# Attention on one core: row maxima from a 36-row product, two matmuls in the two row halves of the array

## The chip, the cores and the metric

The program runs on one core of a Trainium2 chip. The metric is the device time of one execution in microseconds (us), the median of several. TensorE does the matmuls, VectorE reductions and copies, ScalarE exponentials, GpSimd elementwise work; SyncE issues the DMAs.

## The reference

One transformer block with conditioning, in float32: x is [2, 2048, 576], 16 heads of width 36, MLP width 2304.

```
ada = silu(c) @ W_ada + b_ada                       # six shifts, scales and gates
h = layernorm(x) * (1 + scale_msa) + shift_msa
q, k, v = split(h @ W_qkv + b_qkv)                  # 16 heads of 36
attn = softmax(einsum('blhd,bmhd->bhlm', q * 36**-0.5, k))
x = x + gate_msa * (attn @ v @ W_proj + b_proj)
h = layernorm(x) * (1 + scale_mlp) + shift_mlp
x = x + gate_mlp * (gelu(h @ W_fc1 + b_fc1) @ W_fc2 + b_fc2)
```

The change is in the attention: 2 batches of 16 heads make 32 heads, each with a 2048 x 2048 matrix of scores.

## The kernel before

The program runs in phases: `phase_qkv` (to 423 us of the profile), `phase_attention` (424 to 2338 us), `phase_proj`, `phase_mlp`. Every engine has its instructions in program order; they meet in semaphores.

**Operands.** q and k are stored as a high part and a low part (`qkh`, `qkl`). For a head, `qs` and `ks` hold 108 rows: high, low, high of q against high, high, low of k, so one matmul over 108 rows sums the three products. Rows 108 and 109 of `qs` hold the negative row maximum in two parts, against ones in `ks`; a matmul over 110 rows gives the scores less their row maximum. Three heads are held (`NB` = 3).

**Row maxima (units).** `score_max` (line 1207) multiplies 128 queries with 512 keys over 108 rows into one of four PSUM banks `sp`; VectorE's `tensor_reduce` (line 1269) takes the maximum over the 512. A head has 64 units. They run ahead: `THERE` = 80 units are done in `phase_qkv`, the other 1968 in attention, eight in a batch. When a head's units are done, `row_max`, a transpose on TensorE (line 1213) and two small operations on VectorE make the two rows of maxima, which SyncE writes into `qs`.

**Scores.** `scores_t` (line 1224) multiplies 128 keys with 512 queries over 110 rows into one of three banks `st`; ScalarE's exponential (line 1326) writes `pt`. Tile x goes to bank x % 3. `bank_free` makes its weight load wait until the exponential of tile x - 3 is done. From tile `X0`, when no units are left, the scores have six banks.

**Value products.** `products` (line 1237) multiplies 128 keys by 37 columns of v (36 and a one for the sum) with two halves of `pt`, the pair (a = 0, 1) in the column halves of the array, into one bank `op`. Each matmul is float32 and stands in the trace as two records. After eight pairs (a block) ScalarE and VectorE copy the bank out (lines 1334 and 1302), GpSimd adds the halves, SyncE stores them.

**Order.** The list `plan` sets the order on every engine. A batch b is eight score tiles. TensorE runs unit, score, unit, score, ... (eight of each), and then the four value products (16 records) of batch b - 1. There are 256 batches; 246 of them carry units.

Of the kernel before, what the change touches and what calls it, by code (L numbers as in the profile page):

```python
# [7 lines left out]
F = mybir.dt.float32  # L8
# [8 lines left out]
H = 16  # L17
# [12 lines left out]
NH = B * H  # L30

# [353 lines left out]
def phase_qkv(nc, A, ident, adaT, eps, bq, sc, qs0, ks0, qs1, ks1, hh0, lo0, mx, nm, mh, ml, gd, xf, cond, W_ada,  # L385
# [127 lines left out]
    def sync(e):  # L513
# [59 lines left out]
        def first_loads():  # L573
            e.wait_ge(s_on, 3)
            e.wait_ge(s_qo[0], 32 * tiles_before(HCH * NF))
            e.wait_ge(s_qo[1], 32 * tiles_before(HCH * NF + 1))
            for dst, src, r in ((qs0, qkh, 0), (qs0, qkl, 36), (qs0, qkh, 72), (ks0, qkh, 0), (ks0, qkh, 36),
                                (ks0, qkl, 72)):
                f0 = C if dst is ks0 else 0
                e.dma_start(dst[r:r + D, :].bitcast(F), src[f0:f0 + D, 0:L]).then_inc(s_q0, 16)  # L580

        def second_loads():
            e.wait_ge(s_mm, UN * (NCH - 1))
            e.wait_ge(s_q0, 96)
            e.dma_start(ks1[108:110, :].bitcast(F), ks0[108:110, :].bitcast(F)).then_inc(s_q1, 16)
            for dst, src, r in ((qs1, qkh, 0), (qs1, qkl, 36), (qs1, qkh, 72), (ks1, qkh, 0), (ks1, qkh, 36),
                                (ks1, qkl, 72)):
                f0 = D + (C if dst is ks1 else 0)
                e.dma_start(dst[r:r + D, :].bitcast(F), src[f0:f0 + D, 0:L]).then_inc(s_q1, 16)
# [50 lines left out]
        e.wait_ge(s_q0, 96)  # L640
        e.wait_ge(s_q1, 112)
        e.wait_ge(s_m, 32)

    def tensor(e):
# [33 lines left out]
        def score_max(n):  # L678
            h, k = divmod(n, 64)
            qb, k4, q, kk = k // 4, k % 4, (qs0, qs1)[h], (ks0, ks1)[h]  # L680
            if n < 2:
                e.wait_ge(s_row, 12)
                e.wait_ge(s_q0, 96)
            else:
                e.wait_ge(s_mx, n - 1)
            if n == 64:
                e.wait_ge(s_mh, 2)
                e.wait_ge(s_q1, 112)
            e.matmul(sp[n % 2][:, :], q[0:108, qb * 128:qb * 128 + 128], kk[0:108, k4 * 512:k4 * 512 + 512],
                     start=True, stop=True).then_inc(s_s, 1)  # L690
# [329 lines left out]
def phase_attention(nc, A, W, tile, ident, qs0, ks0, qs1, ks1, mx, nm, mh, ml, gd, W_proj, b_proj, xf, qkh, qkl, vd,  # L1020
# [12 lines left out]
    NP = 8  # L1033
    G = NH * 32
    NBAT = G // 4
    NBLK = G // 8
    W0 = 24
    LAST = NBAT - 8
    INV = NBLK // 2 + 6
    THERE = 80  # L1040
    X0 = 64 * NH - THERE
# [3 lines left out]
    ks = [ks0, ks1, A.sb("ks2", [128, L], R)]  # L1045
    vs = [A.sb(f"vs{i}", [128, 16, VW]) for i in range(2)]
# [4 lines left out]
    sp = [A.ps(f"sp{i}", [128, 512]) for i in range(4)]  # L1051
# [11 lines left out]
    for b in range(NBAT + 1):  # L1063
        s = Step()
        s.b, s.last = b, None
        s.late = plan[-1].last if plan else None
        s.slot = None
        if s.late is not None:
            s.slot = len(slots)
            slots.append(("mh", s.late))  # L1070
        s.units = [[] for _ in range(8)]
        for i in range(min(8, NH * 64 - todo)):
            s.units[i].append((todo, len(slots)))
            slots.append(("mx", todo))
            todo += 1
            if todo % 64 == 0:
                s.last = todo // 64 - 1
        s.turn = b - LAST - 1 if LAST < b <= LAST + KT else None
        s.now = b - 1 if 0 < b <= NBAT else None
        s.block = (b - 3) // 2 if b > 2 and b % 2 else None  # L1080
        plan.append(s)

    def slot_free(e, k):

        if k > 3:
            kind, n = slots[k - 4]
# [6 lines left out]
    spare = (len(slots) - 1) % 4  # L1093
    six = [st[(X0 + j) % 3] for j in range(3)] + [sp[j] for j in range(4) if j != spare]

    def bank(x):

        return st[x % 3] if x < X0 else six[(x - X0) % 6]

    def bank_free(e, x):  # L1100
        if x < X0 + 3:
            if x > 2:
                e.wait_ge(s_p, x - 2)
        elif x < X0 + 6:
# [12 lines left out]
    def weight(b):  # L1117

        j, r = divmod(b - W0, 4)
        return divmod(j, KT) if 0 <= j < 2 * KT and r == 0 else (None, None)  # L1120

    def sync(e):
        def load(h):
            i, b, hd = h % NB, h // H, h % H
            sl = slice(b * L, (b + 1) * L)
            if h >= NB:
                e.wait_ge(s_st, 64 * (h - 2))
            if h == H:
                tile.stored(e)
            for dst, src, r in ((qs, qkh, 0), (qs, qkl, 36), (qs, qkh, 72), (ks, qkh, 0), (ks, qkh, 36),  # L1130
                                (ks, qkl, 72)):
                f0 = hd * D + (C if dst is ks else 0)
                e.dma_start(dst[i][r:r + D, :].bitcast(F), src[f0:f0 + D, sl]).then_inc(s_qk[i], 16)
# [12 lines left out]

        load_v(0)
# [6 lines left out]
        for s in plan:  # L1154
# [7 lines left out]
            if s.b < NBAT:  # L1162
                h, r = divmod(s.b, 8)
                if r == 0 and h + 2 < NH:
                    load(h + 2)
                if r == 2 and h + 1 < NH:
                    load_v(h + 1)
# [19 lines left out]
        for i in range(NB):  # L1187
            e.wait_ge(s_qk[i], 96 * len(range(i, NH, NB)) - (96 if i < 2 else 0))
            e.wait_ge(s_m[i], 32 * len(range(i, NH, NB)) - (32 if i == 0 else 0))
        e.wait_ge(s_one, 16)  # L1190
# [10 lines left out]
    def tensor(e):  # L1201
        def score_max(n, slot):
            h, k = divmod(n, 64)
            qb, k4, i = k // 4, k % 4, h % NB
            loaded(e, h)
            slot_free(e, slot)
            e.matmul(sp[slot % 4][:, :], qs[i][0:108, qb * 128:qb * 128 + 128], ks[i][0:108, k4 * 512:k4 * 512 + 512],  # L1207
                     start=True, stop=True).then_inc(s_s, 1)

        def max_rows(h, slot):  # L1210
            e.wait_ge(s_nm, h)
            slot_free(e, slot)
            e.transpose(sp[slot % 4][0:16, 0:128], nm[:, :], ident[:, :]).then_inc(s_mt, 1)

        def scores_t(x):
            h, u, kb = x // 64, (x // 16) % 4, x % 16
            i = h % NB
            if x % 64 == 0:
                if h == 2:
                    e.wait_ge(s_one, 16)  # L1220
                loaded(e, h)
                rows_there(e, h)
            bank_free(e, x)
            e.matmul(bank(x)[:, :], ks[i][0:110, kb * 128:kb * 128 + 128], qs[i][0:110, u * 512:u * 512 + 512],  # L1224
# [16 lines left out]
        def turn(kt):  # L1241
# [5 lines left out]
            e.matmul(sp[spare][:, :], W.sel[:, kt, :], W.rr[:, 0, :], start=True, stop=True).then_inc(W.s_ta, 1)  # L1247

        for s in plan:
            if s.late is not None:  # L1250
                max_rows(s.late, s.slot)
            for q in range(8):
                for n, slot in s.units[q]:
                    score_max(n, slot)
                if s.b < NBAT:
                    scores_t(8 * s.b + q)
            if s.turn is not None:
                turn(s.turn)
            if s.now is not None:
                for q in range(4):  # L1260
                    products(4 * s.now + q)

    def vector(e):
        def score_max(n, slot):
            k = n % 64
            e.wait_ge(s_s, n - THERE + 1)
            if k < 2:
                e.wait_ge(s_nm, n // 64 - 1)
            e.tensor_reduce(mx[:, k // 4, k % 4:k % 4 + 1], sp[slot % 4][:, :], AX.X, ALU.max).then_inc(s_mx, 1)  # L1269

        def row_max(h):
            e.wait_ge(s_mx, 64 * (h + 1) - THERE)
# [21 lines left out]
        for s in plan:  # L1294
            if s.late is not None:
                max_rows(s.late, s.slot)
# [6 lines left out]
            for q in range(8):  # L1303
                if (s.b, q) == (0, 5):
                    tile.low(e)
                for n, slot in s.units[q]:
                    score_max(n, slot)
                    if n % 64 == 63:
                        row_max(n // 64)
# [4 lines left out]
            if s.turn is not None:  # L1314
                e.wait_ge(W.s_ta, s.turn + 1)
                e.wait_ge(W.s_a[0], 48)
                e.tensor_tensor(W.oi[:, s.turn, :], sp[spare][:, :], W.oi[:, s.turn, :], ALU.mult).then_inc(
                    W.s_u, 1)

    def scalar(e):  # L1320
        def exps(x):
# [4 lines left out]
            e.activation(pt[g % NP][:, a * 512:a * 512 + 512], bank(x)[:, :], ACT.Exp, scale=SCALE).then_inc(s_p, 1)  # L1326

        for s in plan:
# [20 lines left out]
    def gpsimd(e):  # L1349
# [36 lines left out]
        for s in plan:  # L1386
# [820 lines left out]
```

## Time and profile before

| | |
|---|---|
| median of 3 runs | 3413.26 us (3413.03 to 3413.68) |
| profiled execution, from first to last instruction | 3411.2 us |
| granted TensorE clock | 1.00 throughout |
| TensorE busy | 3398.5 us |
| VectorE busy | 1978.2 us |
| ScalarE busy | 1498.0 us |
| attention with units (246 batches) | 424.03 to 2275.51 us |
| attention without units | 2275.51 to 2338.31 us |

The profile gives for the profiled execution the span only; all runs lie 1.8 to 2.5 us above it. A matmul's recorded length holds its way through the array, so two of them in a row overlap in the records: what a matmul costs is the distance between the starts of two neighbours.

### The profile page before, as it was taken

How to read it: one execution, taken by the hardware profiler on the slowest of the kernel's cores; microseconds unless marked ns; L12 is line 12 of the kernel's file. 1: busy time of each engine (PE TensorE's matmuls, PEld its weight loads, DVE VectorE, ACT ScalarE, POOL GpSimd, SP SyncE). 2: the span in 40 equal slices, each digit the busy share in tenths (PEclk: the TensorE clock that was granted, in tenths of full speed). 3: DMA queues.
4: the chain of work that ended last, by engine and by line, in shares of the span. 5: the costliest groups of instructions: out<-in, count | busy, mean ns of one | idle time of the engine just before them, and what ended most of it. 6: DMA issues, size and time to landing. Idle time of an engine off the chain costs nothing. (4 is left out here: it accounts for less than half of the span.)

```text
span 3411.2 us, 46656 instructions
## 1 busy us (share of the span) xinstructions
PE 3398.5 (100%) x17032; PEld 2270.5 (67%) x17032; DVE 1978.2 (58%) x3591; ACT 1498.0 (44%) x2806; POOL 361.5 (11%) x283
## 2 busy tenths in 40 slices
PE   9999999999999999999999999999999999999999
PEld 7888845545545545544554554547988989898988
DVE  6447577766776776776776676754643343423332
ACT  3322355555555555555555555566531111212120
POOL 0000010111100000010000000015610101000000
PEclk9999999999999999999999999999999999999999
DMA  7563421212112121111212112114751212421211
GB/s 230 177 186 115 153 74 30 65 41 61 38 34 51 31 55 30 45 43 33 55 31 51 34 31 54 31 39 153 267 173 51 80 49 91 126 84 47 76 55 53
DMA packets 132596, 266.15 MB, mean 78 GB/s; under 512 B 17475, under 2 KB 39491, under 8 KB 125458
## 3 DMA queue, kind: packets, MB, share of 16 engines
q1 hardware_dynamic: 132374, 263.17, 25.8%
q8 instruction: 142, 2.33, 0.3%
q14 instruction: 80, 0.66, 0.1%
HBM read 164.64 MB, written 97.26 MB: 77 GB/s over the span
## 5 line engine op out<-in xcount | busy, mean ns | idle before, releaser
L1269 DVE TENSOR_REDUCE q_mx<-b_sp 128x1 f32<-128x512 f32 x1968 | 1196.4, 676 | 228.2 <-PE b_sp L1207 228.2
L1326 ACT ACTIVATE b_pt<-b_st 128x512 f32<-128x512 f32 x2009 | 1013.4, 626 | 441.5 <-PE b_st L1224 434.2
L1237 PE MATMUL b_op<-b_pt,b_vs 128*37 128x512 f32 x4096 | 929.4, 596 | 0.0
L1237 PEld LDWEIGHTS b_op<-b_pt,b_vs 128*37 128x37 f32 x4096 | 223.7, 113 | 567.5 <-issue 440.4
L2073 PE MATMUL d_pm<-d_vh,d_ah 128*128 128x288 f32 x1152 | 339.3, 295 | 0.6 <-DVE d_al L2111 0.6
L2074 PE MATMUL d_pm<-d_vl,d_ah 128*128 128x288 f32 x1152 | 339.3, 295 | 0.0
L2075 PE MATMUL d_pm<-d_vh,d_al 128*128 128x288 f32 x1152 | 339.2, 294 | 0.0
L1392 POOL TENSOR_TENSOR w_oc<-b_oa,b_ob 37x512 f32<-37x512 f32 x127 | 163.0, 1284 | 1589.1 <-DVE b_ob L1302 1583.1
L1207 PE MATMUL b_sp<-q_hh,q_lo 108*128 108x512 f32 x688 | 284.1, 413 | 0.9 <-PEq L1011 0.9
L1224 PE MATMUL b_st<-q_qs,q_ks 110*128 110x512 f32 x697 | 275.7, 397 | 0.0
L1224 PE MATMUL b_st<-q_lo,q_hh 110*128 110x512 f32 x672 | 263.9, 397 | 0.0
L1207 PE MATMUL b_sp<-q_ks,q_qs 108*128 108x512 f32 x640 | 263.7, 412 | 0.0
L1207 PE MATMUL b_sp<-b_ks,b_qs 108*128 108x512 f32 x640 | 263.7, 412 | 0.0
L1302 DVE COPY b_ob<-b_op 37x512 f32<-37x512 f32 x127 | 86.7, 683 | 292.4 <-PE b_op L1237 292.4
L1224 PE MATMUL b_st<-b_qs,b_ks 110*128 110x512 f32 x640 | 253.3, 396 | 0.0
L1334 ACT ACTIVATE b_oa<-b_op 37x512 f32<-37x512 f32 x127 | 75.6, 595 | 347.9 <-PE b_op L1237 347.9
L2073 PEld LDWEIGHTS d_pm<-d_vh,d_ah 128*128 128x128 f32 x1152 | 216.1, 188 | 1.5 <-issue 0.9
L2074 PEld LDWEIGHTS d_pm<-d_vl,d_ah 128*128 128x128 f32 x1152 | 216.1, 188 | 0.7
L2075 PEld LDWEIGHTS d_pm<-d_vh,d_al 128*128 128x128 f32 x1152 | 216.2, 188 | 0.0
L2122 DVE TENSOR_TENSOR d_ug<-d_pm,d_gt 128x288 f32<-128x288 f32 x128 | 58.5, 457 | 243.3 <-PE d_pm L2075 243.2
L1207 PEld LDWEIGHTS b_sp<-q_hh,q_lo 108*128 108x128 f32 x688 | 130.1, 189 | 103.1 <-issue 76.2
L1207 PEld LDWEIGHTS b_sp<-q_ks,q_qs 108*128 108x128 f32 x640 | 121.1, 189 | 94.1 <-issue 71.1
(415 smaller groups left out, 4665.9 us busy)
## 6 DMA issues: line engine op xcount, KB each, us to landing
qkh<-a_th SPq DMA_DIRECT2D x72, 256.0 KB, 2.0
qkl<-a_tl SPq DMA_DIRECT2D x72, 256.0 KB, 2.1
d_yi<-y SPq DMA_DIRECT2D x64, 288.0 KB, 3.0
n_oi<-hw SPq DMA_DIRECT2D x12, 1024.0 KB, 5.8
vd<-a_vx SPq DMA_DIRECT2D x8, 1184.0 KB, 6.6
b_vs<-vd SPq DMA_DIRECT2D x32, 296.0 KB, 2.8
a_x<-in_x SPq DMA_DIRECT2D x8, 1152.0 KB, 6.4
ot<-w_oc SPq DMA_DIRECT2D x128, 72.0 KB
```

The costliest lines, as they stand in the source:

```text
L1207: e.matmul(sp[slot % 4][:, :], qs[i][0:108, qb * 128:qb * 128 + 128], ks[i][0:108, k4 * 512:k4 * 512 + 512], start=True, stop=True).then_i ...
L1224: e.matmul(bank(x)[:, :], ks[i][0:110, kb * 128:kb * 128 + 128], qs[i][0:110, u * 512:u * 512 + 512], start=True, stop=True).then_inc(s_st, 1)
L1237: ins = e.matmul(op[64 * a:64 * a + VW, :], vs[h % 2][:, 2 * j + a, :], pt[g % NP][:, a * 512:a * 512 + 512], start=j == 0, stop=j == 7)
L1269: e.tensor_reduce(mx[:, k // 4, k % 4:k % 4 + 1], sp[slot % 4][:, :], AX.X, ALU.max).then_inc(s_mx, 1)
L1302: e.tensor_copy(ob[i][:, :], op[0:VW, :]).then_inc(s_oa, 1)
L1326: e.activation(pt[g % NP][:, a * 512:a * 512 + 512], bank(x)[:, :], ACT.Exp, scale=SCALE).then_inc(s_p, 1)
L1334: e.activation(oa[i][:, :], op[64:64 + VW, :], ACT.Copy).then_inc(s_oa, 1)
L1392: e.tensor_tensor(oc[i][:, :], oa[i][:, :], ob[i][:, :], ALU.add).then_inc(s_oc, 1)
L2073: e.matmul(out, ah[:, f, ts], vh[:, f, cs], start=f == 0, stop=False)
L2074: e.matmul(out, ah[:, f, ts], vl[:, f, cs], start=False, stop=False)
L2075: ins = e.matmul(out, al[:, f, ts], vh[:, f, cs], start=False, stop=f == NT - 1)
L2122: e.tensor_tensor(ug[m % 2][:, :], pm[m % 4][:, 0:HALF], gt[:, b, cs], ALU.mult).then_inc(s_ug, 1)
```

## The change

- `rows_of` orders the 108 rows anew: high q against high k stands in rows 0 to 35, high q against low k in rows 64 to 99, and low q against high k in rows 36 to 63 and 100 to 107. A head takes eight DMAs where it took six. A ninth loads `km`: the high part of k for keys 1024 to 2047, in rows 64 to 99 (two buffers). Its wait in `load` is for the units of the head that used the buffer.
- A unit is now 128 queries by 1024 keys in two matmuls over 36 rows: rows 0 to 35 of `qs` with `ks` (the first 1024 keys), rows 64 to 99 of `qs` with `km` (the second 1024). They write the two banks of one PSUM tile `sp2` of 1024 columns. One `tensor_reduce` takes both maxima. The maximum is that of the high parts' product alone. A head has 32 units. 40 are there before attention (`phase_qkv` still makes them with 80 matmuls over 108 rows), 984 are left.
- `sp` was four banks for four units; `sp2` is two tiles for two units. The scores keep their three banks, the value products their one.
- `plan` goes in half-batches hb of four score tiles: TensorE runs two units, four scores, and the two value products of hb - 1. There are 512 half-batches; hb 1 to 492 carry units. `NP`, the number of `pt` buffers, is 6 where it was 8.

On TensorE, within a head in the middle of attention (`b_sp` banks of the units, `b_st` banks of the scores with their number, `b_s_p` the exponentials' semaphore). Before, a piece of a batch's sixteen:

```order
L1207 MATMUL b_sp0<-q_ks0,q_qs0 128x512 [waits b_s_mx,b_s_qk0]
L1224 MATMUL b_st1<-b_qs2,b_ks2 128x512 [waits b_s_p]
L1207 MATMUL b_sp1<-q_ks0,q_qs0 128x512 [waits b_s_mx,b_s_qk0]
L1224 MATMUL b_st2<-b_qs2,b_ks2 128x512 [waits b_s_p]
L1207 MATMUL b_sp2<-q_ks0,q_qs0 128x512 [waits b_s_mx,b_s_qk0]
L1224 MATMUL b_st0<-b_qs2,b_ks2 128x512 [waits b_s_p]
L1207 MATMUL b_sp3<-q_ks0,q_qs0 128x512 [waits b_s_mx,b_s_qk0]
L1224 MATMUL b_st1<-b_qs2,b_ks2 128x512 [waits b_s_p]
```

Units and scores alternated, and two instructions for scores never stood together. At the same place now, a whole half-batch:

```order
L1230 MATMUL b_sp0<-q_ks0,q_qs0 128x512 [waits b_s_mx,b_s_qk0]
L1231 MATMUL b_sp0<-b_km1,q_qs0 128x512
L1230 MATMUL b_sp1<-q_ks0,q_qs0 128x512 [waits b_s_mx,b_s_qk0]
L1231 MATMUL b_sp1<-b_km1,q_qs0 128x512
L1248 MATMUL b_st1<-b_qs2,b_ks2 128x512 [waits b_s_p]
L1248 MATMUL b_st2<-b_qs2,b_ks2 128x512 [waits b_s_p]
L1248 MATMUL b_st0<-b_qs2,b_ks2 128x512 [waits b_s_p]
L1248 MATMUL b_st1<-b_qs2,b_ks2 128x512 [waits b_s_p]
L1261 MATMUL b_op<-b_pt0,b_vs0 37x512 [waits b_s_p]
L1261 MATMUL b_op<-b_pt0,b_vs0 37x512
L1261 MATMUL b_op<-b_pt1,b_vs0 37x512 [waits b_s_p]
L1261 MATMUL b_op<-b_pt1,b_vs0 37x512
```

The two units (lines 1230 and 1231) come first, the four scores follow one another, and the fourth goes to the bank of the first (`b_st1`; its wait for `b_s_p` is for that bank's exponential). Then come two value products, each of two matmuls.

On VectorE, at the same place (`b_ob` is the copy of a block), before:

```order
L1302 COPY b_ob0<-b_op 37x512 [waits b_s_oc,b_s_pv]
L1269 TENSOR_REDUCE q_mx<-b_sp3 128x1 [waits b_s_s]
L1269 TENSOR_REDUCE q_mx<-b_sp0 128x1 [waits b_s_s]
L1269 TENSOR_REDUCE q_mx<-b_sp1 128x1 [waits b_s_s]
L1269 TENSOR_REDUCE q_mx<-b_sp2 128x1 [waits b_s_s]
L1269 TENSOR_REDUCE q_mx<-b_sp3 128x1 [waits b_s_s]
```

and now:

```order
L1325 COPY b_ob0<-b_op 37x512 [waits b_s_oc,b_s_pv]
L1293 TENSOR_REDUCE q_mx<-b_sp0 128x2 [waits b_s_s]
L1293 TENSOR_REDUCE q_mx<-b_sp1 128x2 [waits b_s_s]
L1293 TENSOR_REDUCE q_mx<-b_sp0 128x2 [waits b_s_s]
L1293 TENSOR_REDUCE q_mx<-b_sp1 128x2 [waits b_s_s]
```

Four reductions of one bank each have become two of two banks each; the wait is for the unit's second matmul.

The diff, cut to its core:

```diff
-    NP = 8
+    NP = 6
     G = NH * 32
-    NBAT = G // 4
+    NHB = G // 2
...
-    THERE = 80
-    X0 = 64 * NH - THERE
+    THERE = 40
...
+    km = [A.sb(f"km{i}", [128, L // 2], R) for i in range(2)]
     pt = [A.sb(f"pt{i}", [128, 1024]) for i in range(NP)]
     st = [A.ps(f"st{i}", [128, 512]) for i in range(3)]
     op = A.ps("op", [128, 512])
-    sp = [A.ps(f"sp{i}", [128, 512]) for i in range(4)]
+    sp2 = [A.ps(f"sp{i}", [128, 1024]) for i in range(2)]
+    sp = [sp2[i // 2][:, i % 2 * 512:i % 2 * 512 + 512] for i in range(4)]
...
+            for dst, src, f0, n, r in rows_of(qs[i], ks[i], qkh, qkl, hd * D, C + hd * D):
+                e.dma_start(dst[r:r + n, :].bitcast(F), src[f0:f0 + n, sl]).then_inc(s_qk[i], 16)
+            if h > 2:
+                e.wait_ge(s_s, 32 * (h - 1) - THERE)
+            load_km(h, s_qk[i])
...
         def score_max(n, slot):
-            e.matmul(sp[slot % 4][:, :], qs[i][0:108, qb * 128:qb * 128 + 128], ks[i][0:108, k4 * 512:k4 * 512 + 512],
-                     start=True, stop=True).then_inc(s_s, 1)
+            e.matmul(sp[slot % 2 * 2], qs[i][0:D, queries], ks[i][0:D, keys], start=True, stop=True)
+            e.matmul(sp[slot % 2 * 2 + 1], qs[i][64:64 + D, queries], km[h % 2][64:64 + D, keys], start=True,
+                     stop=True).then_inc(s_s, 1)
...
         for s in plan:
-            if s.late is not None:
-                max_rows(s.late, s.slot)
-            for q in range(8):
-                for n, slot in s.units[q]:
-                    score_max(n, slot)
-                if s.b < NBAT:
-                    scores_t(8 * s.b + q)
+            for n, slot in s.units:
+                score_max(n, slot)
+            if s.hb < NHB:
+                for q in range(4):
+                    scores_t(4 * s.hb + q)
+            if s.late is not None:
+                max_rows(s.late, s.slot)
             if s.turn is not None:
                 turn(s.turn)
             if s.now is not None:
-                for q in range(4):
-                    products(4 * s.now + q)
+                for q in range(2):
+                    products(2 * s.now + q)
...
-            e.tensor_reduce(mx[:, k // 4, k % 4:k % 4 + 1], sp[slot % 4][:, :], AX.X, ALU.max).then_inc(s_mx, 1)
+            e.tensor_reduce(mx[:, k // 2, k % 2 * 2:k % 2 * 2 + 2],
+                            sp2[slot % 2][:, :].rearrange("p (a t) -> p a t", a=2), AX.X, ALU.max).then_inc(s_mx, 1)
```

## Rows read from the trace of the kernel before

**Rows 1.** Page: busy us of each engine, its share of the span, instructions.

```profile
PE 3398.5 (100%) x17032; PEld 2270.5 (67%) x17032; DVE 1978.2 (58%) x3591; ACT 1498.0 (44%) x2806; POOL 361.5 (11%) x283
```

**Rows 2.** Stretches of attention, with and after row maxima: engines' busy us, clock, DMA.

```profile
424.03:2275.51 1851.48, 1851.39 (x7887) 926.42 (x7888) 1295.74 (x2183) 1070.93 (x2103) 193.79 (x151) 1.00 0.17 43
2275.51:2338.31 62.80, 62.31 (x264) 24.78 (x263) 9.72 (x18) 45.88 (x91) 18.22 (x14) 1.00 0.15 47
```

**Rows 3.** Waits from 432 to 2275 us: who for whom, us, times, longest.

```profile
ACT b_pt L1326 <- PE b_st L1224: 428.2, 122, 3.6
...
PEld b_sp L1207 <- DVE q_mx L1269: 0.6, 2, 0.3
```

**Rows 4.** Timeline, TensorE, one batch: start us, length us, instruction.

```profile
790.75 0.50 PE L1207 MATMUL b_sp<-q_hh,q_lo 108*128 108x512 f32 x1
...
791.33 0.40 PE L1207 MATMUL b_sp<-q_hh,q_lo 108*128 108x512 f32 x1
...
793.67 0.39 PE L1207 MATMUL b_sp<-q_hh,q_lo 108*128 108x512 f32 x1
...
794.73 3.63 PE L1237 MATMUL b_op<-b_pt,b_vs 128*37 128x512 f32 x16
798.29 0.50 PE L1207 MATMUL b_sp<-q_hh,q_lo 108*128 108x512 f32 x1
```

**Rows 5.** Timeline, weight loads of that batch's value products.

```profile
795.19 0.12 PEld L1237 LDWEIGHTS b_op<-b_pt,b_vs 128*37 128x37 f32 x2 [0.31 <-ACT b_pt L1326]
...
797.33 0.12 PEld L1237 LDWEIGHTS b_op<-b_pt,b_vs 128*37 128x37 f32 x2 [0.31 <-issue]
```

**Rows 6.** Timeline, TensorE, late stage: matmuls in 64-row halves between full ones.

```profile
2562.32 0.40 PE L2052 MATMUL n_pf<-e_ah,z_wm 128*128 128x512 f32 x1
2562.64 0.50 PE L2028 MATMUL n_pf<-e_ah,e_wr 64*128 64x512 f32 x1
2562.65 0.49 PE L2031 MATMUL d_pm<-e_wh,e_wr 64*128 64x512 f32 x1
2562.98 0.39 PE L2028 MATMUL d_pm<-e_ah,e_wr 64*128 64x512 f32 x1
...
2563.22 0.38 PE L2028 MATMUL d_pm<-e_ah,z_wr 64*128 64x512 f32 x1
...
2563.54 0.50 PE L2052 MATMUL n_pf<-e_ah,z_wh 128*128 128x512 f32 x1
2563.88 0.39 PE L2052 MATMUL n_pf<-q_qs,z_wh 128*128 128x512 f32 x1
```

**Rows 7.** Timeline, scores without row maxima between them: first matmul, first exponential.

```profile
2298.80 0.50 PE L1224 MATMUL b_st<-q_lo,q_hh 110*128 110x512 f32 x1
...
2299.34 0.60 ACT L1326 ACTIVATE b_pt<-b_st 128x512 f32<-128x512 f32 x1 [1.36 <-PE b_st L1224]
```

**Rows 8.** Timeline, weight loads: a score held for an exponential, three banks.

```profile
425.89 0.19 PEld L1224 LDWEIGHTS b_st<-q_qs,q_ks 110*128 110x128 f32 x1 [0.40 <-ACT b_pt L1326]
```

**Rows 9.** Timeline, ScalarE, the exponential that it waits for.

```profile
425.25 1.08 ACT L1326 ACTIVATE b_pt<-b_st 128x512 f32<-128x512 f32 x2
```

**Rows 10.** Timeline, weight loads: a held score, then value products.

```profile
2283.05 0.19 PEld L1224 LDWEIGHTS b_sp<-q_qs,q_ks 110*128 110x128 f32 x1 [0.30 <-ACT b_pt L1326]
2283.48 0.15 PEld L1237 LDWEIGHTS b_op<-b_pt,b_vs 128*37 128x37 f32 x4 [0.24 <-issue]
```

**Rows 11.** Groups of the page: mean ns of one, idle before.

```profile
L1269 DVE TENSOR_REDUCE q_mx<-b_sp 128x1 f32<-128x512 f32 x1968 | 1196.4, 676 | 228.2 <-PE b_sp L1207 228.2
...
L1302 DVE COPY b_ob<-b_op 37x512 f32<-37x512 f32 x127 | 86.7, 683 | 292.4 <-PE b_op L1237 292.4
...
L1334 ACT ACTIVATE b_oa<-b_op 37x512 f32<-37x512 f32 x127 | 75.6, 595 | 347.9 <-PE b_op L1237 347.9
```

**Rows 12.** Line 1275, the reduction over 64 elements: ns min/median/max.

```profile
L1275 DVE TENSOR_REDUCE q_nm<-q_mx x31: 219/219/221, 464.8 to 2273.6; 128x16 f32<-128x64 f32 x31
```

**Rows 13.** One DMA issue of a head's loads on SyncE.

```profile
1503.51 0.37 SPq L1133 DMA_DIRECT2D b_qs<-qkl  x1
```

More of the change, by code:

```diff
@@ L576, in first_loads @@
             e.wait_ge(s_qo[1], 32 * tiles_before(HCH * NF + 1))
[L577 to L580, printed above, removed]
+            for dst, src, f0, n, r in rows_of(qs0, ks0, qkh, qkl, 0, C):
+                e.dma_start(dst[r:r + n, :].bitcast(F), src[f0:f0 + n, 0:L]).then_inc(s_q0, 16)
         def second_loads():
             e.wait_ge(s_mm, UN * (NCH - 1))
-            e.wait_ge(s_q0, 96)
+            e.wait_ge(s_q0, 128)
             e.dma_start(ks1[108:110, :].bitcast(F), ks0[108:110, :].bitcast(F)).then_inc(s_q1, 16)
[L586 to L589, printed above, removed]
+            for dst, src, f0, n, r in rows_of(qs1, ks1, qkh, qkl, D, C + D):
+                e.dma_start(dst[r:r + n, :].bitcast(F), src[f0:f0 + n, 0:L]).then_inc(s_q1, 16)
         def max_rows():
@@ L1062, in phase_attention @@
     todo = THERE
-    for b in range(NBAT + 1):
+    for hb in range(NHB + 1):
         s = Step()
-        s.b, s.last = b, None
+        s.hb, s.last = hb, None
+        s.b = hb // 2 if hb % 2 == 0 else None
         s.late = plan[-1].last if plan else None
+        s.units = []
+        for _ in range(min(2 if hb else 0, 32 * NH - todo)):
+            s.units.append((todo, len(slots)))
+            slots.append(("mx", todo))
+            todo += 1
+            if todo % 32 == 0:
+                s.last = todo // 32 - 1
         s.slot = None
@@ L1070, in phase_attention @@
             slots.append(("mh", s.late))
[L1071 to L1080, printed above, removed]
+            X0 = 4 * (hb + 1)
+        s.turn = s.b - LAST - 1 if s.b is not None and LAST < s.b <= LAST + KT else None
+        s.now = hb - 1 if hb else None
+        s.block = (hb - 5) // 4 if hb > 4 and hb % 4 == 1 else None
         plan.append(s)
     def slot_free(e, k):
-        if k > 3:
-            kind, n = slots[k - 4]
+        if k > 1:
+            kind, n = slots[k - 2]
             if kind == "mx":
@@ L1090, in slot_free @@
                 e.wait_ge(s_mh, 2 * n)
-    spare = (len(slots) - 1) % 4
-    six = [st[(X0 + j) % 3] for j in range(3)] + [sp[j] for j in range(4) if j != spare]
+    spare = 2 * ((len(slots) - 1) % 2)
+    six = [st[(X0 + j) % 3][:, :] for j in range(3)] + [sp[j] for j in range(4) if j != spare]
     def bank(x):
-        return st[x % 3] if x < X0 else six[(x - X0) % 6]
+        return st[x % 3][:, :] if x < X0 else six[(x - X0) % 6]
     def bank_free(e, x):
@@ L1117, in weight, with before @@
     def weight(b):
-        j, r = divmod(b - W0, 4)
+        j, r = divmod(b - W0, 4) if b is not None else (-1, 0)
         return divmod(j, KT) if 0 <= j < 2 * KT and r == 0 else (None, None)
+    def before(s, n):
+        return None if s.b is None else s.b - n
     def sync(e):
@@ L1129, in load, with load_km @@
                 tile.stored(e)
[L1130 to L1133, printed above, removed]
+            for dst, src, f0, n, r in rows_of(qs[i], ks[i], qkh, qkl, hd * D, C + hd * D):
[3 more added lines that the diff above has]
+            load_km(h, s_qk[i])
+        def load_km(h, sem):
+            b, hd = divmod(h, H)
+            e.dma_start(km[h % 2][64:64 + D, :].bitcast(F),
+                        qkh[C + hd * D:C + hd * D + D, b * L + L // 2:(b + 1) * L]).then_inc(sem, 16)
         def load_v(h):
@@ L1187, in sync @@
         for i in range(NB):
-            e.wait_ge(s_qk[i], 96 * len(range(i, NH, NB)) - (96 if i < 2 else 0))
+            e.wait_ge(s_qk[i], 144 * len(range(i, NH, NB)) - (144 if i < 2 else 0))
             e.wait_ge(s_m[i], 32 * len(range(i, NH, NB)) - (32 if i == 0 else 0))
-        e.wait_ge(s_one, 16)
+        e.wait_ge(s_one, 32)
         for i in range(2):
@@ L1212, in max_rows @@
             slot_free(e, slot)
-            e.transpose(sp[slot % 4][0:16, 0:128], nm[:, :], ident[:, :]).then_inc(s_mt, 1)
+            e.transpose(sp[slot % 2 * 2][0:16, 0:128], nm[:, :], ident[:, :]).then_inc(s_mt, 1)
         def scores_t(x):
@@ L1223, in scores_t @@
             bank_free(e, x)
-            e.matmul(bank(x)[:, :], ks[i][0:110, kb * 128:kb * 128 + 128], qs[i][0:110, u * 512:u * 512 + 512],
+            e.matmul(bank(x), ks[i][0:110, kb * 128:kb * 128 + 128], qs[i][0:110, u * 512:u * 512 + 512],
                      start=True, stop=True).then_inc(s_st, 1)
@@ L1246, in turn @@
                 e.wait_ge(W.s_u, kt)
-            e.matmul(sp[spare][:, :], W.sel[:, kt, :], W.rr[:, 0, :], start=True, stop=True).then_inc(W.s_ta, 1)
+            e.matmul(sp[spare], W.sel[:, kt, :], W.rr[:, 0, :], start=True, stop=True).then_inc(W.s_ta, 1)
         for s in plan:
+            for n, slot in s.units:
+                score_max(n, slot)
+            if s.hb < NHB:
+                for q in range(4):
+                    scores_t(4 * s.hb + q)
             if s.late is not None:
                 max_rows(s.late, s.slot)
-            for q in range(8):
-                for n, slot in s.units[q]:
-                    score_max(n, slot)
-                if s.b < NBAT:
-                    scores_t(8 * s.b + q)
             if s.turn is not None:
@@ L1302, in vector @@
                 e.tensor_copy(ob[i][:, :], op[0:VW, :]).then_inc(s_oa, 1)
[L1303 to L1309, printed above, removed]
+            if s.hb == 0:
+                tile.low(e)
+            for n, slot in s.units:
+                score_max(n, slot)
+                if n % 32 == 31:
+                    row_max(n // 32)
+            if s.late is not None:
+                max_rows(s.late, s.slot)
             if s.block == INV:
@@ L1316, in vector @@
                 e.wait_ge(W.s_a[0], 48)
-                e.tensor_tensor(W.oi[:, s.turn, :], sp[spare][:, :], W.oi[:, s.turn, :], ALU.mult).then_inc(
+                e.tensor_tensor(W.oi[:, s.turn, :], sp[spare], W.oi[:, s.turn, :], ALU.mult).then_inc(
                     W.s_u, 1)
@@ L1334, in scalar @@
                 e.activation(oa[i][:, :], op[64:64 + VW, :], ACT.Copy).then_inc(s_oa, 1)
-            if s.b < NBAT:
-                if s.b == 0:
+            if s.hb < NHB:
+                if s.hb == 0:
                     tile.evict(e)
-                for q in range(8):
-                    exps(8 * s.b + q)
+                for q in range(4):
+                    exps(4 * s.hb + q)
             if s.block == INV + 1:
                 W.high(e, 0)
-            i, kt = weight(s.b - 2)
+            i, kt = weight(before(s, 2))
             if i is not None:
@@ L1394, in gpsimd @@
                 W.low(e, 0)
-            i, kt = weight(s.b - 1)
+            i, kt = weight(before(s, 1))
             if i is not None:
                 W.w[i].gate(e, kt, W.stg, W.gt)
-            i, kt = weight(s.b - 2)
+            i, kt = weight(before(s, 2))
             if i is not None:
                 W.w[i].low(e, kt, W.stg)
-            if LAST + 2 <= s.b < LAST + 2 + KT:
+            if s.b is not None and LAST + 2 <= s.b < LAST + 2 + KT:
                 kt = s.b - LAST - 2
```

41 lines of the change are left out of this document (24 added, 17 removed).

## The prediction

> **What bounds the kernel now.** I read five views. The page's busy times come first: TensorE 3398.5 of 3411.2 us, VectorE 58%, ScalarE 44% [rows 1]. That alone does not bind the change to TensorE, since a busy record of it can hold a wait. So I asked for the stretches next. The units run from 424.03 to 2275.51 us: 1851.48 us for 246 batches, 7.53 us each, at a granted clock of 1.00, that is 2.4 GHz; VectorE works 1295.7 and ScalarE 1070.9 us of it [rows 2]. In the waits of this stretch ScalarE waits for scores 428 us, while TensorE's unit loads wait for VectorE 0.6 us, and no wait of a score's weight load for an exponential is listed (the first two stand in [rows 3]). So TensorE sets the pace and is almost never held.
>
> The timeline of one batch shows how its time is made up. The sixteen matmuls of units and scores take 3.98 us (790.75 to 794.73) and the eight value pieces 3.56 us (794.73 to 798.29). Within the sixteen, ten steps from 791.33 to 793.67 are 0.234 us each [rows 4]. Value pieces follow each other in (797.33 - 795.19) / 5 = 0.43 us; each piece is two records side by side [rows 5]. Both groups have edges that cost more than their interior steps, and these decide this case.
>
> **The change, part by part.**
>
> *Units.* The trace has matmuls in row halves, over 64 rows, in the MLP. Two start within 0.01 us (2562.64, 2562.65), the next pair 0.34 later, the next 0.24 later, and the first full matmul 0.32 after the last pair; from the last full matmul to the first pair it is 0.32 too, where two full ones lie 0.234 apart [rows 6]. So a pair costs what one matmul costs, and a change between full and half rows costs about 0.09 before and 0.10 after: the first matmul behind it is 0.50 long with its weight load in sight, and its follower starts 0.34 later. A group of n steps therefore takes 0.34 + 0.234 (n - 2) + 0.32. Check on the sixteen: 3.94, measured 3.98.
>
> The eight units of a batch, 8 x 0.234 = 1.87 us, become four pairs in two groups. A group of two is 0.34 + 0.32 = 0.66 us. The records are over 64 rows, the new ones over 36; I take the same, and bound it from above by no overlap at all (the rival below).
>
> *Scores.* Four in a row, if nothing held them: 0.34 + 2 x 0.234 + 0.32 = 1.13 us. But they have three banks, and the fourth's weight load waits for the exponential of the first. Chain: first matmul 0.50 (2298.80), exponential starts 0.04 after its end (2299.34) and lasts 0.60 [rows 7]. The release is read at the one place where three banks did hold a score: exponential from 425.25 [rows 9], weight load at 425.89 [rows 8], 0.64 later. Together 0.54 + 0.64 = 1.18 us from the start of the group. Unheld, the fourth matmul would start at 0.34 + 2 x 0.234 = 0.81. From a held weight load to the value products it is 0.43 (2283.05 to 2283.48) [rows 10], since the load is now in sight. The group takes 1.18 + 0.43 = 1.61 us, 0.48 more than unheld. Before, three scores lay 3 x 0.468 = 1.40 us apart from the fourth through the units between them, more than 1.18, and so hid the same exponential. That cover is what the new order takes away. Nothing in the half-batch can fill it: behind the held load stand only the fourth score and the value products, in order, and their data have long been there. From above I bound the wait by a longer exponential: two in a row took 1.08 [rows 9], 0.54 each with their overlap, so I allow 0.05 more than 0.60. From below the weight load could be hidden: 0.11 less.
>
> *Value products.* Two in a group instead of four: 3.56 - 4 x 0.43 = 1.84 us.
>
> A half-batch is 0.66 + 1.61 + 1.84 = 4.11 us, a pair of them 8.22, against 7.53 before. Without the hold it would be 3.63, or 7.26.
>
> The edges go from two in a batch to six; the four more cost 4 x 0.1, of the 0.94 that four pairs for eight steps save, and the two holds take 0.96.
>
> *VectorE.* A reduction over 512 lasts 0.676 [rows 11], over 64 0.219 [rows 12]: 1.02 ns an element, so 1.20 us for 1024 as an estimate, and two of them 2.4 us of 4.11; a copy of 0.68 comes every fourth half-batch [rows 11]. It would bind above about (4.11 - 0.2) / 2 = 1.95 us for one. From above two old reductions are 1.35, so neither end binds. A pair of reductions starts at about 0.5 us and ends before 3.0, and the next half-batch needs the tile at 4.1. ScalarE has four exponentials and a quarter of a copy, 2.2 us. Its copy of a block comes in the first 0.8 us of a half-batch, before the first score is done at 0.66 + 0.50, so it is hidden; were it not, it would cost 128 x 0.6 at the most.
>
> The Trainium skill, "TensorEngine Tiling (Array Packing)", section PSUM Bottleneck, speaks against this change here: a faster TensorE leaves the emptying of PSUM as the possible bound. By that rule the kernel would come out as in the last rival below; by the rows VectorE has 1.5 us of each half-batch to spare, since the hold slows TensorE more than the pairs speed it up.
>
> *DMA and SyncE.* Three more issues a head at 0.37 [rows 13], 1.1 us in 66, on a queue whose next work is a store. The wait in front of `km` is for units that the plan finishes four half-batches earlier. Behind it stand stores of a block, for which GpSimd waits only two blocks later. The units of that head begin 13 half-batches later. Price nothing, uncovered 1.1 us a head, 35 us in all. At the start, TensorE's second half-batch needs `km` and the ones; I take 3.5 us for half-batch 0 with the landing.
>
> *Row maxima's way.* The transpose comes three half-batches before the head's scores, 12 us, where two batches gave 15. The two DMAs need some 3 us, hidden.
>
> *End.* After the units: one held half-batch (1.61 + 1.84 + 0.1), 18 with six banks of 1.13 + 1.84, five extra matmuls of 0.234, the last value group 1.84 and 0.5 to the next phase, 60.6 us against 62.8 [rows 2].
>
> *Sum.* 3.5 + 492 x 4.11 + 30 transposes of 0.1 = 2028.6, against 1851.5: +177. The end gives 2 back: +175. I add 0.02 for each half-batch, the part by which the measured sixteen exceed their formula (0.04 a batch), +10: +185. The profiled execution is 3411.2, so 3596 is the new span, and with 2.1 us around it 3598 for the median (3413.3 before).
>
> **Rivals.**
>
> *No overlap of the halves over 36 rows.* Each pair is then two steps: 2 x 0.234 x 492 = +230, 3828 us. Against it stand the 0.01 us between the starts over 64 rows [rows 6] and the two column halves of the value products.
>
> *The hold costs nothing* (not slower). If the fourth score went on as in before, where three banks also served and no such wait is listed, a half-batch would be 3.63 + 0.02 and the kernel 3598 - 492 x 0.48 = 3362 us, faster. The place is the fourth weight load, the price 0.48; it turns the sign when the hold is below (7.53 / 2 - 3.65) = 0.12 us. For it: the cover is usual in this kernel. Against it: the exponential alone is 0.60, and the code names the bank.
>
> *The units at half price and nothing else.* The Trainium skill, "TensorEngine Tiling (Array Packing)", section Overview, gives up to two times for a contraction of at most 64 rows. As a mechanism of this kernel: eight steps a batch become four, edges and hold free, 246 x 4 x 0.234 = 230 less, 3183 us. The edges of rows 6 speak against it.
>
> *VectorE binds.* At 2.1 us for a reduction over two banks a half-batch is 2 x 2.1 + 0.17 = 4.37: 3710 us. Rows 11 and 12 are far below it.
>
> **Chances.** Forecast (held, overlapped) 0.89; no overlap 0.05; hold free 0.02; half price 0.01; VectorE binds 0.03. The forecast's own range is 492 x (-0.11 to +0.05) around 3598, 3544 to 3623; the low end needs every held load hidden, which rows 10 deny, so 3560. Above I leave room for more edges than counted, 0.1 a half-batch: 3650. What this kernel's measurement can tell from no change is about 0.2%, 7 us. Faster 0.03, within 0.2% 0.01 (a hold near 0.12), slower 0.96.
>
> **What would show it.** The fourth score's weight load should stand with an idle time of some 0.4 us ascribed to the exponential, about 490 times; the two matmuls of a unit should start within 0.02 us; starts of half-batches should lie 4.1 us apart; reductions should be 1.1 to 1.4 us long, with VectorE's idle ended by units; the clock should stay at 2.4 GHz. The prediction is wrong if the pair is staggered by 0.2 us or more, or if the fourth score starts less than 1.0 us after the first.

## The result, and the profile after

The changed kernel takes 3599.14 us (median of 4 runs, 3597.78 to 3600.6) against 3413.15 for the kernel before, run beside it (4 runs): ratio 1.0546, 95% interval 1.0531 to 1.0561. The forecast was 3598. The profiled execution spans 3598.1 us.

Two rows of the page: busy time of each engine, and the new reduction.

```profile
PE 3470.6 (96%) x17032; PEld 2015.2 (56%) x17032; DVE 1937.1 (54%) x2607; ACT 1523.7 (42%) x2806; POOL 359.7 (10%) x283
...
L1293 DVE TENSOR_REDUCE q_mx<-b_sp 128x2 f32<-128x1024 f32 x984 | 1156.7, 1216 | 622.3 <-PE b_sp L1231 622.3
```

TensorE's records fill 3470.6 us, 72 more than before [rows 1], although the units have half as much array time; VectorE works 41 us less. A reduction over 1024 columns lasts 1.216 us; the estimate was 1.20.

Stretches of attention (us; busy us of TensorE, its weight loads, VectorE, ScalarE, GpSimd; clock; DMA share, GB/s), with units and after them, as [rows 2] has them of before:

```profile
424.44:2463.36 2038.92, 1926.45 (x7906) 674.31 (x7906) 1255.78 (x1199) 1097.83 (x2107) 191.55 (x151) 1.00 0.19 42
2463.36:2524.07 60.71, 59.80 (x244) 21.74 (x243) 9.20 (x18) 44.88 (x87) 18.21 (x14) 1.00 0.09 27
```

With units it is 2038.92 us for 1851.48, at the same granted clock of 1.00. TensorE is now without a record for 112 us of it; before, 0.1. The end is 60.71 for 62.80. The whole loss lies in the first stretch.

Waits from 432 to 2460 us, who for whom, us, times, longest:

```profile
DVE q_mx L1293 <- PE b_sp L1231: 620.0, 367, 4.5
...
PEld b_st L1248 <- ACT b_pt L1350: 321.7, 490, 0.7
...
PE b_st L1248 <- ACT b_pt L1350: 109.6, 490, 0.2
...
PE b_sp L1230 <- DVE q_mx L1293: 0.3, 1, 0.3
```

A score's weight load waits for an exponential 490 times; the same list of the kernel before, of which [rows 3] shows two lines, has no such wait. Its idle time, 321.7 / 490 = 0.66 us, is that of the loader, which ended the third score's load long before; TensorE itself stands without a record for 0.22 us of it, since a record holds a matmul's whole way through the array. The cost is neither of the two: it is read from the starts. VectorE waits for units 620 us, and the units wait for VectorE once, 0.3 us, so VectorE does not bind.

One half-batch in the timeline (start us, length us, instruction; idle before and its releaser):

```profile
1500.59 0.49 PE L1230 MATMUL b_sp<-b_ks,b_qs 36*128 36x512 f32 x1
...
1500.60 0.49 PE L1231 MATMUL b_sp<-b_km,b_qs 36*128 36x512 f32 x1
...
1500.93 0.39 PE L1230 MATMUL b_sp<-b_ks,b_qs 36*128 36x512 f32 x1
...
1501.25 0.96 PE L1248 MATMUL b_st<-q_lo,q_hh 110*128 110x512 f32 x3
1501.79 2.06 ACT L1350 ACTIVATE b_pt<-b_st 128x512 f32<-128x512 f32 x4 [2.05 <-PE b_st L1248]
1502.44 0.19 PEld L1248 LDWEIGHTS b_st<-q_lo,q_hh 110*128 110x128 f32 x1 [0.66 <-ACT b_pt L1350]
...
1502.88 1.92 PE L1261 MATMUL b_op<-b_pt,b_vs 128*37 128x512 f32 x8
...
1504.72 0.50 PE L1230 MATMUL b_sp<-b_ks,b_qs 36*128 36x512 f32 x1
```

The two matmuls of a unit start within 0.01 us. The units' group lasts 0.66 (1500.59 to 1501.25), the scores' 1.63, of which 1.19 to the held weight load, the products' 1.84. The next half-batch starts 4.13 us after this one.

The same trace has this group without the wait. After the last unit the scores have six banks:

```profile
2467.14 0.96 PE L1248 MATMUL b_st<-q_qs,q_ks 110*128 110x512 f32 x3
2467.94 0.40 PE L1248 MATMUL b_sp<-q_qs,q_ks 110*128 110x512 f32 x1
2468.27 1.91 PE L1261 MATMUL b_op<-b_pt,b_vs 128*37 128x512 f32 x8
```

Four scores between value products take 1.13 us there (2467.14 to 2468.27, and in the mean of 13 such groups), against 1.615 in the mean of those with units. The wait costs 0.49 us a half-batch, some 240 us in all. Without it two half-batches would take 2 x (0.666 + 1.13 + 1.849) = 7.29 us for the 7.53 of a batch before: the halves, less the added edges, are worth some 59 us, and the wait takes four times that.

### The profile page after: what moved, and what is told of

Its sections match the earlier page's. It is cut to its first block and busy times, and to the rows that moved or that the text cites. A ratio compares the mean times of both kernels' runs of the same rounds, so it can differ in the third digit from the quotient of the medians.

```text
span 3598.1 us, 44809 instructions
## 1 busy us (share of the span) xinstructions
PE 3470.6 (96%) x17032; PEld 2015.2 (56%) x17032; DVE 1937.1 (54%) x2607; ACT 1523.7 (42%) x2806; POOL 359.7 (10%) x283
## 5 line engine op out<-in xcount | busy, mean ns | idle before, releaser
L1293 DVE TENSOR_REDUCE q_mx<-b_sp 128x2 f32<-128x1024 f32 x984 | 1156.7, 1216 | 622.3 <-PE b_sp L1231 622.3
L1350 ACT ACTIVATE b_pt<-b_st 128x512 f32<-128x512 f32 x2012 | 1039.7, 603 | 834.6 <-PE b_st L1248 834.5
L1261 PE MATMUL b_op<-b_pt,b_vs 128*37 128x512 f32 x4096 | 981.9, 600 | 0.0
L1261 PEld LDWEIGHTS b_op<-b_pt,b_vs 128*37 128x37 f32 x4096 | 201.4, 113 | 444.6 <-issue 366.0
L1248 PEld LDWEIGHTS b_st<-q_qs,q_ks 110*128 110x128 f32 x701 | 118.2, 188 | 189.0 <-ACT b_pt L1350 115.9
L1248 PEld LDWEIGHTS b_st<-q_lo,q_hh 110*128 110x128 f32 x671 | 112.8, 187 | 180.3 <-ACT b_pt L1350 113.4
L1248 PEld LDWEIGHTS b_st<-b_qs,b_ks 110*128 110x128 f32 x640 | 107.5, 187 | 170.4 <-ACT b_pt L1350 105.0
L2186 ACT ACTIVATE d_af<-n_pf,q_mx 128x512 f32<-128x512 f32 x80 | 55.1, 689 | 217.9 <-PE d_pm L2055 164.3
L989 ACT ACTIVATE a_tf<-a_pm,g_bq 128x512 f32<-128x512 f32 x71 | 48.9, 688 | 210.6 <-PE a_pm L709 193.7
L1230 PEld LDWEIGHTS b_sp<-q_hh,q_lo 36*128 36x128 f32 x344 | 50.9, 185 | 145.8 <-issue 144.1
```

The source lines that it names most:

```text
L1248: e.matmul(bank(x), ks[i][0:110, kb * 128:kb * 128 + 128], qs[i][0:110, u * 512:u * 512 + 512], start=True, stop=True).then_inc(s_st, 1)
L1261: ins = e.matmul(op[64 * a:64 * a + VW, :], vs[h % 2][:, 2 * j + a, :], pt[g % NP][:, a * 512:a * 512 + 512], start=j == 0, stop=j == 7)
L1293: e.tensor_reduce(mx[:, k // 2, k % 2 * 2:k % 2 * 2 + 2], sp2[slot % 2][:, :].rearrange("p (a t) -> p a t", a=2), AX.X, ALU.max).then_inc( ...
L1350: e.activation(pt[g % NP][:, a * 512:a * 512 + 512], bank(x), ACT.Exp, scale=SCALE).then_inc(s_p, 1)
L2186: e.activation(af[m % 2][:, :], bank(n, f)[:, :], ACT.Gelu_apprx_tanh, bias=b1[:, half * NT + f:half * NT + f + 1]).then_inc(s_af, 1)
```

## The experiments

The theory: the order, not the row halves, makes the loss; four scores in a row on three banks wait 0.48 us for the first one's exponential, and each further group edge costs 0.1 to 0.2. The rivals: the halves or their edges make the loss, the overlap is poor, or VectorE does.

**The fourth score behind the products.**

```diff
-                for q in range(4):
+                for q in range(3):
                     scores_t(4 * s.hb + q)
...
                 for q in range(2):
                     products(2 * s.now + q)
+            if s.hb < NHB:
+                scores_t(4 * s.hb + 3)
```

> The fourth score of each half-batch is moved behind the two value products, so the exponential of the first score runs beside them. Theory (the hold on the fourth score costs 0.48 us, each further group edge about 0.19): units 0.66 + three scores 0.34 + 0.234 + 0.32 = 0.89 + products 1.84 + one score 0.43 = 3.83 us a half-batch for 4.13, 492 x 0.30 = 148 less than 3599: 3451 us, and no score load waits for an exponential. Rival (the hold is incidental; edges between row halves and full rows, or VectorE, set the pace): one more edge, so the same or up to 492 x 0.1 = 50 more, 3599 to 3650 us.

Measured: 3476.41 us, ratio to before 1.0189 (1.0159 to 1.0218), 123 less than the changed kernel, with one edge more in each half-batch. The timeline of TensorE, and the weight load of the fourth score:

```profile
1500.39 0.50 PE L1230 MATMUL b_sp<-q_ks,q_qs 36*128 36x512 f32 x1
...
1501.05 0.96 PE L1248 MATMUL b_st<-b_qs,b_ks 110*128 110x512 f32 x3
1501.95 1.92 PE L1261 MATMUL b_op<-b_pt,b_vs 128*37 128x512 f32 x8
1503.79 0.19 PEld L1248 LDWEIGHTS b_st<-b_qs,b_ks 110*128 110x128 f32 x1 [0.83 <-ACT b_pt L1352]
1503.79 0.50 PE L1248 MATMUL b_st<-b_qs,b_ks 110*128 110x512 f32 x1
1504.22 0.49 PE L1230 MATMUL b_sp<-q_ks,q_qs 36*128 36x512 f32 x1
```

Three scores take 0.90, the products 1.84, the single score 0.43, the units 0.66: 3.83, as expected. The rival falls. The fourth score now costs its edge, 0.90 + 0.43 - 1.13 = 0.20 us, in place of the wait of 0.49.

No score load was expected to wait for an exponential, and the list of waits (440 to 2300 us) seems to deny it:

```profile
PEld b_st L1248 <- ACT b_pt L1352: 379.5, 455, 0.8
```

These are the loader's idle times behind the value products, 0.83 us each. The units' first load stands idle for the same 0.83 behind the same products in the changed kernel, where nothing is waited for, and the list has no wait of TensorE itself for an exponential, where the changed kernel has 490. The exponential that the list names costs nothing here.

The 25 us above the forecast are elsewhere: the group of three scores is 0.90 ahead of products and 1.25 ahead of a transpose of row maxima (means over all of them in the trace), plus 0.20 for the transpose itself. So 30 transposes cost 0.55 each where the changed kernel has 0.11 (its held score hides them): 13 us. At the end some groups wait too (mean 1.43 for 1.19, 18 times, 4 us), and the mean half-batch is 0.01 to 0.02 longer than its terms.

**Both matmuls of a unit in the same row half.**

(`late_keys` are the same 512 of the second 1024 keys.)

```diff
-            e.matmul(sp[slot % 2 * 2 + 1], qs[i][64:64 + D, queries], km[h % 2][64:64 + D, keys], start=True,
+            e.matmul(sp[slot % 2 * 2 + 1], qs[i][0:D, queries], ks[i][0:D, late_keys], start=True,
                      stop=True).then_inc(s_s, 1)
```

> Both matmuls of a unit use rows 0 to 35, so they cannot run side by side; all else stays. If the pairs overlap in full in the changed kernel, the group of units grows from two steps to four, 0.66 to 1.13 us, 492 x 0.468 = 230 more: 3829 us. Rival (the pairs hardly overlap, and the loss was in them): 3599 to 3650 us.

Measured: 3829.61 us (one run). In TensorE's timeline the four matmuls of two units start one after another:

```profile
1500.98 0.50 PE L1230 MATMUL b_sp<-q_ks,q_qs 36*128 36x512 f32 x1
1501.32 0.39 PE L1232 MATMUL b_sp<-q_ks,q_qs 36*128 36x512 f32 x1
1501.55 0.39 PE L1230 MATMUL b_sp<-q_ks,q_qs 36*128 36x512 f32 x1
1501.78 0.39 PE L1232 MATMUL b_sp<-q_ks,q_qs 36*128 36x512 f32 x1
1502.10 0.96 PE L1249 MATMUL b_st<-b_qs,b_ks 110*128 110x512 f32 x3
1503.29 0.49 PE L1249 MATMUL b_st<-b_qs,b_ks 110*128 110x512 f32 x1 [0.22 <-ACT b_pt L1351]
```

The group is 1.12 us (1500.98 to 1502.10) for 0.66; the scores behind it are held as before. 492 x 0.46 = 226 of the 230 us. So a pair side by side costs what one matmul costs: the overlap of the halves over 36 rows is whole.

**Units over all 108 rows in the new order.**

```diff
-            e.matmul(sp[slot % 2 * 2], qs[i][0:D, queries], ks[i][0:D, keys], start=True, stop=True)
-            e.matmul(sp[slot % 2 * 2 + 1], qs[i][64:64 + D, queries], km[h % 2][64:64 + D, keys], start=True,
+            e.matmul(sp[slot % 2 * 2], qs[i][0:108, queries], ks[i][0:108, keys], start=True, stop=True)
+            e.matmul(sp[slot % 2 * 2 + 1], qs[i][0:108, queries], ks[i][0:108, late_keys], start=True,
                      stop=True).then_inc(s_s, 1)
```

> A unit is two matmuls over all 108 rows again (keys 0 to 1023 and 1024 to 2047), in the new order and with the new tiles. No row halves, so units and scores are one group with no edge between: the first score starts at 0.34 + 3 x 0.234 = 1.04, its load is hidden (0.40 + 0.04 + 0.64 = 1.08 to the release of the fourth), then 0.43 and products 1.84: 4.39 us a half-batch, 492 x 0.26 = 128 more than 3599: 3727 us. With 8 steps of 0.234 it has the same matmul work as the kernel before (3413), so the excess over it, 314, is the price of the order alone: half-batches (246 x 0.19 = 47) and the hold. Rival (row halves are what costs, the order is free): at or below 3460 us.

Measured: 3731.58 us (one run). TensorE's timeline:

```profile
1499.75 0.50 PE L1231 MATMUL b_sp<-q_hh,q_lo 108*128 108x512 f32 x1
...
1500.79 0.86 PE L1249 MATMUL b_st<-q_qs,q_ks 110*128 110x512 f32 x3
1501.87 0.51 PE L1249 MATMUL b_st<-q_qs,q_ks 110*128 110x512 f32 x1 [0.22 <-ACT b_pt L1351]
1502.31 1.92 PE L1262 MATMUL b_op<-b_pt,b_vs 128*37 128x512 f32 x8
1504.15 0.50 PE L1231 MATMUL b_sp<-q_hh,q_lo 108*128 108x512 f32 x1
```

This kernel has as many matmuls over full rows as the kernel before, and the order, tiles, loads and reductions of the changed one. The order, with the tiles and loads that belong to it, so costs some 318 us, and the halves then give back 132. Of the 318, some 240 are the wait: units and scores together take 2.55 us in the mean, against 0.34 + 6 x 0.234 + 0.32 = 2.06 unheld. Most of the rest is that the groups are half as long (2.06 + 1.85 = 3.91 us for half of 7.53, some 70 us in all). The rival, that the halves are what costs, falls.

**Exponentials of half the columns.**

```diff
-            e.activation(pt[g % NP][:, a * 512:a * 512 + 512], bank(x), ACT.Exp, scale=SCALE).then_inc(s_p, 1)
+            e.activation(pt[g % NP][:, a * 512:a * 512 + 256], bank(x)[:, 0:256], ACT.Exp, scale=SCALE).then_inc(s_p, 1)
```

> The exponential takes 256 of the 512 columns of each tile; the other half of the value product's operand is ones, written once, so half of the softmax is left out. TensorE's instructions stay. Theory: the release of the fourth score comes earlier by what the exponential is shorter, about 256 x 0.95 ns = 0.24 us, so 492 x 0.24 = 118 less: 3481 us, with some 5 us for the writing at the start. Rival (the hold is not what sets the half-batch): 3595 to 3605 us.

Measured: 3496.97 us (one run), 102 less than the changed kernel. One exponential, and the held weight load, in the timeline:

```profile
1499.92 0.38 ACT L1351 ACTIVATE b_pt<-b_st 128x256 f32<-128x256 f32 x1
...
1502.33 1.47 PE L1249 MATMUL b_st<-b_qs,b_ks 110*128 110x512 f32 x4
1502.86 1.35 ACT L1351 ACTIVATE b_pt<-b_st 128x256 f32<-128x256 f32 x4 [2.55 <-PE b_st L1249]
1503.29 0.19 PEld L1249 LDWEIGHTS b_st<-b_qs,b_ks 110*128 110x128 f32 x1 [0.44 <-ACT b_pt L1351]
1503.72 0.15 PEld L1262 LDWEIGHTS b_op<-b_pt,b_vs 128*37 128x37 f32 x4 [0.24 <-ACT b_pt L1351]
```

The load now comes 0.96 us after the group's start (1502.33 to 1503.29) for 1.19. The mean group of scores is 1.40 for 1.615, 492 x 0.212 = 104. The other groups keep their lengths (units 0.665, products 1.849), although the products need exponentials and ScalarE's copies too. So this shows that the hold is for the exponential and passes its length on one for one. The forecast's 0.95 ns a column stands in no row; from 512 to 256 columns the exponential went from 0.60 to 0.38 us, 0.86 ns a column. 0.22 for 0.24 is 10 of the 16 us by which the forecast missed.

**Scores in three, three and two.** Two half-batches are taken together, every three scores have units or products behind them, and ScalarE's copy of a block is put ahead of the fourth exponential.

```diff
+        for s in plan[0::2]:
+            unit_part(s)
...
+            for q in range(3):
+                scores_t(x + q)
+            product_part(s)
+            unit_part(s2)
+            for q in range(3, 6):
+                scores_t(x + q)
+            product_part(s2)
+            for q in range(6, 8):
+                scores_t(x + q)
```

> Units in row halves are kept; two half-batches are taken together and the eight scores stand in groups of three, three and two, each with units or value products between, so no score has to wait for an exponential (the copy of a block on ScalarE is moved ahead of the fourth exponential). Theory of edges and hold: 2 x 0.66 + 2 x 0.89 + 0.66 + 2 x 1.84 = 7.45 us for eight scores, against 7.53 in the kernel before and 8.26 in the changed one; the end without units has more edges and gives back some 4 us. 3413 - 246 x 0.08 + 4 = 3397 us, a little faster than before, 5.6% faster than the changed kernel. Rival (the halved units are worth more than counted, 0.94 us a batch, once the hold is gone): below 3300. Rival (the edges cost more than counted): 3430 and above.

Measured: 3425.38 us, ratio to before 1.0037 (1.0024 to 1.0051), so 0.4% slower, where faster was expected. The groups are as expected (0.66, 0.89, 1.85, 0.66, 0.89, 1.85, 0.66; their means add up to 7.47 us), but not where a transpose of row maxima stands between scores and products:

```profile
1503.46 0.27 PE L1237 MATMUL b_sp<-g_ident,q_nm 128*16 128x128 f32 x1 [0.45 <-DVE q_mx L1308]
1503.66 0.63 PE L1261 MATMUL b_op<-b_pt,b_vs 128*37 128x512 f32 x2
```

It waits for VectorE's reduction of the tile that it writes. A group of three scores ahead of it is 1.42 us long for 0.89 (means), and the transpose adds 0.20: 0.72 us each. In the kernel before, from which the forecast counts, it is 0.12 (0.03 itself, 0.09 in the sixteen matmuls behind it); the difference over 30 is 18 of the 28 us missed. Some 6 more are the groups' means, 7.47 for the 7.45 counted. The rest is not settled.

**The same with the transpose behind the products.** It stands ahead of the last two scores, and the end without units goes in groups of four scores again.

```diff
             product_part(s2)
+            if s2.late is not None:
+                max_rows(s2.late, s2.slot)
             for q in range(6, 8):
```

> As the version with scores in three, three and two, whose trace shows that the 30 transposes of row maxima wait about 0.65 us each for VectorE there. Here a transpose stands behind the second pair of value products, ahead of the two scores, when its tile has long been free; and the end without units goes in groups of four scores again. Theory: 30 x 0.65 = 20 and some 3 us at the end less than 3425: 3402 us, 0.3% faster than the kernel before. Rival (the distance of that version to its forecast of 3397 lies in the groups' edges, not in the transposes): 3420 to 3425 us.

Measured: 3410.24 us (11 runs), ratio to before 0.9995, interval 0.9986 to 1.0004: no difference from before can be told. It is 15 us faster than the version above. One transpose and its neighbours:

```profile
2276.28 0.28 PE L1238 MATMUL b_sp<-g_ident,q_nm 128*16 128x128 f32 x1
...
2276.32 0.94 PE L1249 MATMUL b_st<-q_qs,q_ks 110*128 110x512 f32 x3
2276.60 0.28 DVE L1331 CAST q_mh<-b_sp 16x128 fp32r<-16x128 f32 x1 [2.25 <-PE b_sp L1238]
...
2276.91 0.28 DVE L1333 TENSOR_TENSOR q_ml<-b_sp,q_mh 16x128 fp32r<-16x128 f32 x1
```

The transpose costs 0.03 us here. Of the 8 us missed, some 5 are units behind a transpose, which wait for the two small operations of VectorE on its tile (the units' group after two scores is 0.68 in the mean, 0.66 else). The rest is not settled.

**That order with units over 108 rows.** The edit is that of the third experiment.

> As the previous kernel (scores in three, three and two), but a unit is two matmuls over all 108 rows. Units and scores then share a mode: 16 steps of 0.234 + 8 value pieces of 0.43 + 4 groups of 0.19 = 7.94 us for eight scores, against 7.47 with row halves: 246 x 0.47 = 116 more than the previous kernel, about 3518 us. That would be what the halves are worth once no score is held. Rival (the halves are worth nothing, edges eat it all): the same time as the previous kernel.

Measured: 3491.49 us (one run), 81 more than with row halves. So the halves are worth 81 us in an order that fits them, not 116: the means of the groups add up to 7.83 us for eight scores, not 7.94, against 7.50 in the kernel with row halves. The forecast gave each group 0.19 for its edges; 0.19 is right for groups of scores and units, but the products' have 1.85 - 4 x 0.43 = 0.13, and two of the four groups are products.

## Why the prediction was right

*The half-batch.* Forecast 0.66 + 1.61 + 1.84 = 4.11; means over the trace 0.666 + 1.615 + 1.849 = 4.13. The 0.02 added for what the formula left out was the right size by luck: it was read from the sixteen alternating matmuls, a group that the changed kernel does not have. From the first score to the end of the last half-batch with units 2038.6 was forecast; it is 2038.92.

*Units.* The rows of the MLP's matmuls over 64 rows [rows 6] carried over to 36 rows to the hundredth. The same-half experiment shows the overlap by its loss.

*The hold.* The sum from [rows 7 to 10] gave 1.18 to the release and 0.43 behind it; the timeline has 1.19 and 0.44. Three experiments bear it out: the moved score (123 us back in spite of an edge), the shorter exponential (102 back), and the order without halves (318 us lost, some 240 of them to the wait). That the fourth load would show 0.4 us of idle time was read wrongly: it shows 0.66 on the loader and 0.22 on TensorE, and only the starts give 0.49 (1.615 less 1.13).

*VectorE.* Weighed at 1.20 us a reduction and found to have room; 1.216, and 620 us of waiting for units. Its busy share fell from 58 to 54%.

*Start.* 3.5 us were allowed for half-batch 0 and the landing of `km`; the units start 3.72 us after the first score (424.44 to 428.16), held by DMAs at its end.

*End.* 60.6 forecast, 60.71 measured. The remaining 1.6 us of the span lie outside attention.

*Sums that do not add up.* Two, and neither enters the forecast. The prediction has four more edges in a batch at 4 x 0.1, against 0.94 saved and 0.96 for the holds. That gives 0.42 us more a batch, where its own half-batches give 8.22 - 7.53 = 0.69: a group has an edge on both sides, and by the means of the traces the four added groups cost some 0.7 in all, 0.17 each. A reader who priced the change by that sentence would be 66 us short (246 x 0.27). And a half-batch of 4.37 us, in the rival with VectorE, is 3716 us, not 3710.

*Rivals.* The one on the other side, a hold that costs nothing, named the right place: without the hold and with unchanged edges the kernel would be near 3360, an estimate from the 0.49 above. No order tried reached it. In the three orders tried with three banks the hold was traded for more edges, and the best trade ends at the time of the kernel before. A fourth bank for the scores while units run, and pairs of units set singly between scores, were not tried. Of the others, no overlap falls by the starts of the pairs and by the experiment with one half, VectorE binding by the units' one wait for it, 0.3 us, and the units at half price with nothing else by the edges.

## What to carry to other kernels

Running two short contractions side by side in the row halves takes the array time of one (two pairs took 0.66 us with their edges, four in a row 1.12), but each group has an edge of about 0.1 us on either side; count the groups in a period before counting the halved steps. Matmuls of another kind that stand between two uses of a PSUM bank are cover for the engine that empties it: when they are shortened or moved, compare the distance of the two uses in steps with the way matmul, exponential, release. Where an engine is held, take the cost from the distance between starts, not from the idle time shown.

## What the runs showed of the hardware beyond this

- A transpose of 128 x 16 costs 0.03 us between products and scores, and 0.20 between scores and products, on top of any wait for its tile.
- The edges of a group depend on its kind: 0.19 us for groups over full rows or row halves with 128 columns of weights, 0.13 for the value products in column halves with 37.
- An exponential took 0.60 us for 512 columns and 0.38 for 256, so by these two points some 0.16 of it, an estimate, does not shrink with the columns.
- Behind eight records of value products the weight loader stood idle 0.83 us before the next group's first load, whatever that was and whatever it was said to wait for.
